# A four-layer graph transformer on one core: inverted places in the experts' routing, edge products awaited in twos, the output stored by tile

## What is computed

```python
xn = _layernorm(x)
x = x + gnn(xn, edges) + mix(xn)      # one kind of gnn and mix for each layer
x = x + ffn(_layernorm(x))

# layer 0's graph part
msg = edge_val[:, None] * (x @ W.T + b)[edge_col]
agg = segment_sum(msg, edge_row, num_segments=N)

# layer 3's feed-forward part (layer 1 likewise; layer 0 with one expert a node)
rw, re = top_k(softmax(tokens @ router_w.T), 2)      # weights and experts of a node
for e in range(8):
    h = gelu(tokens @ w1[e] + b1[e]); y = h @ w2[e] + b2[e]
    out = out + combine[:, e:e + 1] * y               # zero where e was not chosen
```

## Time and profile before

| | |
|---|---|
| time, median of 3 runs | 6284.4 us (6282.38 to 6292.41) |
| the profiled execution's own time | 6301.26 us |
| its span | 6299.3 us |
| mean granted TensorE clock | 0.798 of full speed |
| TensorE busy (matmul) | 4413.6 us, 70% |
| VectorE busy | 3201.3 us, 51% |
| GpSimd busy | 2895.1 us, 46% |
| ScalarE busy | 1234.3 us, 20% |
| DMA | 623.84 MB, mean 99 GB/s |

### The profile page before, as it was taken

One profiled execution on the slowest core, in us unless ns is written; L12 is line 12 of the kernel. 1 busy time (PEld: TensorE's weight loads), 2 busy tenths in 40 slices (PEclk: granted clock), 3 DMA queues, 4 the chain that ended last, 5 costly groups with the idle time before them and its releaser, 6 DMA issues. The chain is left out here.

```text
span 6299.3 us, 67353 instructions
## 1 busy us (share of the span) xinstructions
PE 4413.6 (70%) x17694; PEld 3077.6 (49%) x17694; DVE 3201.3 (51%) x7674; ACT 1234.3 (20%) x3062; POOL 2895.1 (46%) x2882
## 2 busy tenths in 40 slices
PE   0398857776796677665964937887399986777643
PEld 0246633333585454432444825566267763566542
DVE  7325545555002667777971145788722233577622
ACT  0022200001222110101142311100033342333211
POOL 1456656663101488774853046677100006566233
PEclk9998865556898775657986967988699998889776
DMA  4100013334011699885732224444300003222233
GB/s 154 50 6 2 2 54 92 91 92 112 28 34 58 200 288 284 272 265 159 222 103 74 69 75 121 107 111 112 69 1 0 0 22 102 76 86 87 70 105 106
DMA packets 411510, 623.84 MB, mean 99 GB/s; under 512 B 76713, under 2 KB 304446, under 8 KB 410789
## 3 DMA queue, kind: packets, MB, share of 16 engines
q0 software_dynamic: 124448, 324.61, 18.1%
q1 hardware_dynamic: 283588, 292.22, 14.8%
q10 hardware_dynamic: 3154, 3.20, 0.2%
HBM read 482.93 MB, written 137.50 MB: 98 GB/s over the span
## 5 line engine op out<-in xcount | busy, mean ns | idle before, releaser
L867 POOL DMA_INDIRECT m_rows<-support,far_at x440 | 447.6, 1017 | 1000.6 <-POOLq L126 748.8
L877 PE MATMUL g_sums_bank<-g_sums_rows,g_sums_same 128*125 128x256 f32 x880 | 459.2, 642 | 185.2 <-issue 171.1
L3855 POOL DMA_INDIRECT g_sp_rows<-h,src_at x440 | 467.4, 1062 | 220.1 <-issue 107.3
L3229 POOL DMA_INDIRECT g_sc_rows<-keyval,src_at x440 | 439.4, 999 | 238.1 <-issue 104.7
L522 POOL DMA_INDIRECT records<-record,place_at x416 | 419.2, 1008 | 281.2 <-issue 120.3
L867 POOL DMA_INDIRECT g_sums_rows<-h,far_at x440 | 415.6, 945 | 229.0 <-PE g_sums_bank L877 137.7
L3252 PE MATMUL g_sc_pair<-g1q_parts,g_sc_near 125*128 x1320 | 315.9, 366 | 191.5 <-DVE g_sc_rows L3296 134.9
L877 PEld LDWEIGHTS g_sums_bank<-g_sums_rows,g_sums_same 128*125 128x125 f32 x880 | 215.5, 292 | 428.8 <-issue 406.9
L3904 PE MATMUL g_sp_bank<-g_sp_rows,g_sp_same 128*125 128x264 f32 x880 | 309.6, 456 | 92.0 <-issue 49.0
L910 DVE TENSOR_TENSOR g_total<-g_total,g_sums_bank 125x256 f32 x440 | 184.6, 420 | 317.4 <-PE g_sums_bank L877 244.9
L936 PE MATMUL m_half<-m_rows,m_marks 128*125 128x256 f32 x880 | 254.8, 424 | 111.4 <-issue 72.3
(11 more groups left out here) (706 smaller groups left out, 9960.0 us busy)
## 6 DMA issues: line engine op xcount, KB each, us to landing
kept<-g_sc_rows SPq DMA_DIRECT2D x440, 128.0 KB
g_sp_rows<-kept SPq DMA_DIRECT2D x440, 128.0 KB
xnT<-sorted_rows SPq DMA_DIRECT2D x80, 256.0 KB
answer_rows<-f_answer SPq DMA_DIRECT2D x64, 256.0 KB
g_sc_kind_in<-kind_rows SPq DMA_DIRECT2D x55, 256.0 KB
g_sc_local_in<-local_rows SPq DMA_DIRECT2D x55, 250.0 KB
g_sp_local_in<-local_rows SPq DMA_DIRECT2D x55, 250.0 KB
answer_rows<-zero SPq DMA_DIRECT2D x1, 9856.0 KB
```

The costliest lines, as they stand in the source:

```text
L867: nc.gpsimd.indirect_dma_start(self.rows[:, k, :], None, self.table, bass.IndirectOffsetOnAxis(ap=core.far_at[:, s:s + 1], axis=0)).then_i ...
L877: nc.tensor.matmul(self.halves[s % slots], self.same[:, s % self.RING, :], self.rows[:, s % self.SLOTS, :], start=True, stop=True).then_in ...
L3229: nc.gpsimd.indirect_dma_start(rows[:, k, :], None, table, bass.IndirectOffsetOnAxis(ap=core.src_at[:, s:s + 1], axis=0)).then_inc(gathere ...
L3855: nc.gpsimd.indirect_dma_start(self.rows[:, k, :], None, self.table, bass.IndirectOffsetOnAxis(ap=core.src_at[:, s:s + 1], axis=0)).then_i ...
```

## The change

1. **Routing.** The places are inverted. A node's place is split into a block and a lane (VectorE); two sets of 0/1 masks are made, one over the blocks (`in_block`) and one over the 128 lanes (`in_lane`); GpSimd and ScalarE multiply the block masks by the tile's and the row's number (`spread_pool`, `row_act`); TensorE multiplies lane masks by these, 50 bf16 products for each choice (`invert_pe`), so that a bank holds for each lane and block the number of the node that belongs there. VectorE makes two integer lists of it (`to_at`, `from_at`), with spare rows for padding.
2. **Rows.** SP stores `xn` as it stands, by tile, into `sorted_rows` (now 3200 rows), five tiles at a time. In the experts' loop GpSimd gathers a step's rows in two indirect DMAs of 128, and scatters the answers in two, five steps later (LAG), to a region of `answer_rows` that lies by tile and choice. The scatters ahead of the loop and the gathers behind it are gone. Behind the loop SP loads 125 rows for each tile and choice in a plain DMA, into 16 buffers (8 in layer 0) in the memory of W1.
3. **The output** goes out from layer 3's last loop, one DMA of 125 rows for each tile once its two combines are done, eight tiles behind the loads; the phase `store` is gone.
4. **Layer 3's added rows** are added in five slices, one in each of the loop's first five steps.
5. **Layer 0's edge products** are waited for in twos: for a pair TensorE waits for the second matrix, for the add that frees the second bank, and for both gathers, and then issues both products. Banks, buffers and ring stay.
6. The zero fill covers 3200 and 14592 rows.

The diff, cut to its core:

```diff
+
+
+def tile_rows(table, first, count=1):
+
+    return table[first * W:(first + count) * W, :].rearrange("(t p) d -> p t d", p=W)[0:P]
...
-    def multiply(self, pe, s):
+    def multiply_two(self, pe, s):
         nc = self.core.nc
         slots = len(self.halves)
-        pe.wait_ge(self.matched, s + 1)
-        if s >= slots:
-            pe.wait_ge(self.added, s - slots + 1)
-        pe.wait_ge(self.gathered[s % self.SLOTS], 16 * (s // self.SLOTS + 1))
+        pe.wait_ge(self.matched, s + 2)
+        if s + 1 >= slots:
+            pe.wait_ge(self.added, s - slots + 2)
+        for i in (s, s + 1):
+            pe.wait_ge(self.gathered[i % self.SLOTS], 16 * (i // self.SLOTS + 1))
+        nc.tensor.matmul(self.halves[s % slots], self.same[:, s % self.RING, :], self.rows[:, s % self.SLOTS, :], start=True, stop=True).then_inc(self.summed, 1)
+        s += 1
         nc.tensor.matmul(self.halves[s % slots], self.same[:, s % self.RING, :], self.rows[:, s % self.SLOTS, :], start=True, stop=True).then_inc(self.summed, 1)
...
+        self.place, self.block, self.lane = (sb(n, [P, choices, NT]) for n in ("place", "block", "lane"))
+        self.tile_base = sb("tile_base", [P, choices * NT])
+        self.in_block, self.of_tile, self.of_row = (sb(n, [P, choices, NT, self.blocks], BF16) for n in ("in_block", "of_tile", "of_row"))
+        self.in_lane = lanes
...
+        self.started, self.picked, self.summed, self.tabled = (ph.sem(n) for n in ("started", "picked", "summed", "tabled"))
+        self.block_set, self.lane_set, self.tile_set, self.row_set, self.inverted, self.addressed = (
+            ph.sem(n) for n in ("block_set", "lane_set", "tile_set", "row_set", "inverted", "addressed"))
+
+    def spread_pool(self, pool):
         nc = self.core.nc
         for k in range(self.choices):
-            nc.gpsimd.iota(self.place_at[k][96:W], [[1, NT]], base=EXPERT_STEPS * EXPERT_ROWS + k * 32 * NT, channel_multiplier=NT).then_inc(self.started, 1)
+            pool.wait_ge(self.block_set, k + 1)
+            nc.gpsimd.tensor_tensor(self.of_tile[:, k], self.in_block[:, k], bcast_last(self.tile_base[:, k * NT:(k + 1) * NT], [P, NT, self.blocks]), ALU.mult).then_inc(self.tile_set, 1)
+
+    def row_act(self, act):
+        nc = self.core.nc
+        for k in range(self.choices):
+            act.wait_ge(self.block_set, k + 1)
+            nc.scalar.activation(self.of_row[:, k], self.in_block[:, k], ACT.Copy, scale=self.core.row[0:P, 0:1]).then_inc(self.row_set, 1)
+
+    def invert_pe(self, pe, bank):
+        nc = self.core.nc
+        last = self.choices * NT - 1
+        for k in range(self.choices):
+            pe.wait_ge(self.tile_set, k + 1)
+            pe.wait_ge(self.row_set, k + 1)
+            pe.wait_ge(self.lane_set, k + 1)
+            for t in range(NT):
+                n = k * NT + t
+                nc.tensor.matmul(bank[:, 0:self.blocks], self.in_lane[:, k, t, :], self.of_tile[:, k, t, :], start=n == 0, stop=False)
+                ins = nc.tensor.matmul(bank[:, 0:self.blocks], self.in_lane[:, k, t, :], self.of_row[:, k, t, :], start=False, stop=n == last)
+        ins.then_inc(self.inverted, 1)
+
+    def gather(self, pool, into, block, landed):
+        self.core.nc.gpsimd.indirect_dma_start(into, None, self.core.sorted_rows, bass.IndirectOffsetOnAxis(ap=self.from_at[:, block:block + 1], axis=0)).then_inc(landed, 16)
+
+    def scatter(self, pool, rows, block, landed):
+        self.core.nc.gpsimd.indirect_dma_start(self.core.answer_rows, bass.IndirectOffsetOnAxis(ap=self.to_at[:, block:block + 1], axis=0), rows, None).then_inc(landed, 16)
 
...
             link(nc.vector.tensor_tensor(self.equal[:], self.value[:], self.pick[k][:], ALU.mult))
-            link(nc.vector.tensor_reduce(self.place[k][:], self.equal[:].rearrange("p e t -> p t e"), AX.X, ALU.add))
-            nc.vector.tensor_copy(self.place_at[k][0:P], self.place[k][:]).then_inc(self.placed, 1)
+            link(nc.vector.tensor_reduce(self.place[:, k, :], self.equal[:].rearrange("p e t -> p t e"), AX.X, ALU.add))
+        link(nc.vector.tensor_scalar(self.block[:], self.place[:], 1.0 / W, -(W - 1) / (2.0 * W), ALU.mult, ALU.add))
+        link(nc.vector.tensor_scalar(self.block[:], self.block[:], ROUND, None, ALU.add))
+        link(nc.vector.tensor_scalar(self.block[:], self.block[:], ROUND, None, ALU.subtract))
+        link(nc.vector.scalar_tensor_tensor(self.lane[:], self.block[:], -float(W), self.place[:], ALU.mult, ALU.add))
+        wide, long = [P, NT, self.blocks], [P, NT, W]
+        for k in range(self.choices):
+            nc.vector.tensor_tensor(self.in_block[:, k], bcast_mid(core.ramp[0:P, 0:self.blocks], wide), bcast_last(self.block[:, k, :], wide), ALU.is_equal).then_inc(self.block_set, 1)
+        for k in range(self.choices):
+            nc.vector.tensor_tensor(self.in_lane[:, k], bcast_mid(core.ramp[0:P, :], long), bcast_last(self.lane[:, k, :], long), ALU.is_equal).then_inc(self.lane_set, 1)
         shape = [1, self.steps, EXPERTS]
         link(nc.vector.tensor_tensor(self.passed[:], bcast_mid(self.until[0:1, :], shape), bcast_last(core.ramp[0:1, 0:self.steps], shape), ALU.is_le))
         link(nc.vector.tensor_reduce(self.step_expert[:], self.passed[:], AX.X, ALU.add))
         link(nc.vector.tensor_scalar(self.step_expert[:], self.step_expert[:], float(EXPERTS - 1), None, ALU.min))
         nc.vector.tensor_copy(self.expert_at[:, 0:self.steps], self.step_expert[:]).then_inc(self.tabled, 1)
+        v.wait_ge(self.inverted, 1)
+        link(nc.vector.tensor_tensor(self.found[:], place_bank[:, 0:self.blocks], self.slot[:], ALU.max))
+        nc.vector.tensor_copy(self.to_at[:], self.found[:]).then_inc(self.addressed, 1)
+        link(nc.vector.tensor_scalar(self.slot[:], self.found[:], float(W * self.blocks), None, ALU.subtract))
+        if self.choices == 2:
+            link(nc.vector.tensor_scalar(self.fold[:], self.slot[:], float(W * NT), -float(W * NT), ALU.is_ge, ALU.mult))
+            link(nc.vector.tensor_tensor(self.slot[:], self.slot[:], self.fold[:], ALU.add))
+        link(nc.vector.scalar_tensor_tensor(self.fold[:], self.slot[:], -0.25, self.slot[:], ALU.mult, ALU.max))
+        nc.vector.tensor_copy(self.from_at[:], self.fold[:]).then_inc(self.addressed, 1)
...
                     sp.sem_inc(ph.spent, 1)
+            for g in range(NODE_LOOPS):
+                sp.wait_ge(norm.staged, (g + 1) * BODY)
+                sp.dma_start(tile_rows(core.sorted_rows, g * BODY, BODY), core.xn[:, g * BODY:(g + 1) * BODY, :]).then_inc(stored, 16)
             sp.wait_ge(loaded, nload)
-            sp.wait_ge(scattered, 16 * K * NT)
-            for i in range(LAST + 4):
-                if i < LAST:
-                    if i >= IN:
-                        sp.wait_ge(row_turned, i - IN + 1)
-                    sp.dma_start(rows[:, i % IN], core.sorted_rows[i * ROWS:(i + 1) * ROWS, :].rearrange("(j p) d -> p j d", p=128)).then_inc(row_in[i % IN], 16)
-                if i >= 4:
-                    s = i - 4
-                    sp.wait_ge(y_kept, s + 1)
-                    sp.dma_start(core.answer_rows[s * ROWS:(s + 1) * ROWS, :].rearrange("(j p) d -> p j d", p=128), answer[:, s % OUT]).then_inc(saved[s % OUT], 16)
-
-        @block.gpsimd
-        def _(pool):
-            route.spare(pool)
-            pool.wait_ge(route.placed, K)
-            for t in range(NT):
-                for k in range(K):
-                    nc.gpsimd.indirect_dma_start(core.sorted_rows, bass.IndirectOffsetOnAxis(ap=route.place_at[k][:, t:t + 1], axis=0),
-                                                 core.xw[:, t, :], None).then_inc(scattered, 16)
             for k in range(OUT):
-                pool.wait_ge(saved[k], 16 * len(range(k, LAST, OUT)))
+                sp.wait_ge(saved[k], 32 * len(range(k, LAST, OUT)))
             for n in range(K * NT):
                 t, k = n // K, n % K
                 if n >= BACK:
-                    pool.wait_ge(combined, n - BACK + 1)
-                nc.gpsimd.indirect_dma_start(back[:, n % BACK, :], None, core.answer_rows,
-                                             bass.IndirectOffsetOnAxis(ap=route.place_at[k][:, t:t + 1], axis=0)).then_inc(back_in[n % BACK], 16)
+                    sp.wait_ge(combined, n - BACK + 1)
+                sp.dma_start(back[:, n % BACK, :], tile_rows(core.answer_rows, route.blocks + k * NT + t)[:, 0, :]).then_inc(back_in[n % BACK], 16)
+                if out is not None and n >= BACK and (n - BACK) % K == K - 1:
+                    done = (n - BACK) // K
+                    sp.dma_start(nodes(out)[:, done, :], core.x[:, done, :]).then_inc(sent, 16)
+            if out is not None:
+                for t in range(NT - BACK // K, NT):
+                    sp.wait_ge(combined, K * (t + 1))
+                    sp.dma_start(nodes(out)[:, t, :], core.x[:, t, :]).then_inc(sent, 16)
+                sp.wait_ge(sent, 16 * NT)
+
+        @block.gpsimd
```

(35 more changed lines are left out.)

125 lines of the change are left out of this document (68 added, 57 removed).

## The result

The changed kernel takes 6202.6 us, median of 4 runs (6196.35 to 6209.09), against 6286.6 for the one before on the same chip (4 runs, 6282.38 to 6292.41): a ratio of 0.9872, 95% interval 0.9858 to 0.9887. That is 84 us less. The forecast was 152 less (6132), the range reached from 6098 to 6220. The time lies in the range, at the place of the second case, in which the pairing of layer 0's products does nothing (6207). The upper end of the range came from that case, not from the forecast's own sum (6100 to 6165).

The account below looks back on a forecast made before the run. The prediction found no engine full and took layer 0's matmul-to-add turn as its edge stage's pace. Gains of 75 (pairing), 19 (layer 0's experts), 41 (layer 1) and 17 (layer 3) made 152, so 6132 us; range 6098 to 6220.

Parts of the forecast that it names:

- the forecast's own sum: Whole kernel: 152 us gained, median 6132, own range about 6100 to 6165; chance 0.50.
- The pairing: Layer 0's edge products awaited in twos: 1.31 us a step or GpSimd's 1.25, 67 to 88 gained, 75 taken.
- the step that named the bound: Layer 0's edge stage: the turn from matmul to add and back, 1.43 to 1.45 us, sets the pace, not GpSimd.
- the first rival: Layer 0's edge stage: pairing does nothing, since a pair repeats the memory or semaphore turn; 6207, chance 0.22.
- the sign of being wrong: Layer 0's edge stage: the forecast is wrong if the stage keeps 1.46 us a step.
- Layer 3's head: Last reduce to TensorE's first rows in layer 3: 32.9 us against 74.3, 41 gained.
- Layer 3's loop: Layer 3's experts' loop: four GpSimd transfers bind at 5.05 us a step; 8 allowed for clock dips, 3 for slices.
- a rival of 72 for a clock that falls: Layer 3's experts' loop: GpSimd starves TensorE, slow clock, 7.3 us a step, 72 more, 6204; chance 0.10.
- Tails: After the experts' loops: plain 125-row copies at 1.07 us each; layer 3's tail 27 gained.
- The rival in which the copies use all engines: Tails end at VectorE's pace, some 50 us earlier in layer 3 and 25 in layer 1: 6057, chance 0.04.
- Layers 0 and 1's experts: Inverted routing in both: 19 us gained in layer 0 (12 to 22), 41 in layer 1 (30 to 50).
- The slower case: Layer 0's edge stage: six products in flight for seven, 7/6 as long, 107 us more, 6314; chance 0.06.

Follow-up runs that it names:

- the first pair: The kernel before and the changed kernel, measured and profiled first, on one chip: 6286.6 and 6202.6 us, ratio 0.9872.
- the quick kind: Chips on which the unchanged kernel before takes 5982 to 5985 us; there the whole change measured ratio 0.982.
- the first kind: Chips on which the unchanged kernel before takes 6282 to 6303 us; there the whole change measured ratio 0.9872.
- the run with it at 0.95 and more work: Changed kernel with layer 0's products issued twice, layer 3's experts' loop turns three times, and 128-row tail copies: 6129.5 us, ratio 0.9766 to the kernel before.
- the 128-row run: Changed kernel with the plain copies behind the three experts' loops bringing 128 rows each in place of 125: 5796.5 us, ratio 0.9686 to the kernel before.

## Why the prediction was right or wrong

**The pairing: wrong, by the step that named the bound.** The total fell into the range by the first rival, not by the forecast. I read "TensorE's next product starts 0.10 after an add" and "six steps ahead" as a turn of 1.43 us, and took a part of the turn away. A product that waits for a bank starts after an add whatever makes the adds late. The rows that spoke against it were in the trace: an add may run as soon as one of six finished products is signalled, so with six ahead by their records it isn't the products' start that is late but their signal. I put half the chance nevertheless on 75. Measured: -4.4 in the first pair, +1.9 on the quick kind, and nothing when it is undone there; a step takes 639.4/440 = 1.45 us, which is the sign of being wrong that I had set. The first rival named the outcome and its size (6207 for 6203), with the turn's repetition as its reason, which the runs don't bear out: on the quick kind there is no turn at all, 1.27 us a step is GpSimd's own pace, and the most that anything on TensorE could have given was the 84 us down to it. That 6207 and 6203 lie so near is luck: layer 3 gave 17 less than worked out, and the stages ahead of layer 0's experts and the untouched stretch made it up.

**Layer 3's head: better than the sum.** First rows of TensorE at 26.2 after the last reduce in place of 32.9:

```profile
5887.97 0.57 DVE L1533 TENSOR_REDUCE f_place<-f_equal 125x25 f32<-125x200 f32 x1
...
5891.47 10.38 POOL L1455 TENSOR_TENSOR f_of_tile<-f_in_block,f_tile_base 125x1600 bf16<-125x1600 bf16 x2 [97.78 <-DVE f_in_block L1540]
5892.97 12.23 DVE L1542 TENSOR_TENSOR xnT<-ramp,f_lane 125x3200 bf16<-125x3200 f32 x2
...
5908.47 0.19 DVE L1550 CAST f_to_at<-f_found 128x64 int32<-128x64 f32 x1
...
5910.50 0.99 POOL L1477 DMA_INDIRECT xnT<-sorted_rows,f_from_at  x1 [8.65 <-DVE f_from_at L1556]
...
5914.70 1.09 PE L1806 MATMUL f_bank<-ident,xnT 128*128 128x128 f32 x4 [6.53 <-DMA xnT<-sorted_rows,f_from_at]
```

The masks end at 5905.20, 15.7 after the small ops, where I had 10.2 + 6.5 in series. In series is what the trace shows, though the rows overlap: a row's time holds its wait for the other engine. The second block mask ends at 5893.05 and the first multiply 2.72 later, at 5895.77; the first lane mask ends 3.35 after that, the second multiply 2.73 after the mask, the second lane mask 3.35 after the multiply. So a lane mask of 6.15 by its row is 3.35 of work (3.4 in the sum), and a multiply of 4.3 or 6.1 is 2.7 (3.3 in the sum). Layer 0's experts show the same with one choice:

```profile
1686.12 0.99 DVE L1540 TENSOR_TENSOR f_in_block<-ramp,f_block 125x800 bf16<-125x800 f32 x1
1687.03 3.48 DVE L1542 TENSOR_TENSOR f_hid<-ramp,f_lane 125x3200 bf16<-125x3200 f32 x1
...
1687.27 4.64 POOL L1455 TENSOR_TENSOR f_of_tile<-f_in_block,f_tile_base 125x800 bf16<-125x800 bf16 x1 [203.74 <-DVE f_in_block L1540]
1690.43 1.75 DVE L1544 TENSOR_TENSOR f_passed<-f_until,ramp 1x256 f32<-1x256 f32 x1
```

The mask came first and took its 3.48; the multiply of half the size ends 1.40 after it, and VectorE's next op, 0.41 in layer 3, takes 1.75. The mis-sized term of the head is the second choice's 50 products: 3.0 us, 0.053 each, for the 9.5 that I had from 0.19 each. The row that I took it from has 128 columns at half clock among waits.

**Layer 3's loop: the mechanism right, its size only on the quick kind.** Four transfers a step bind the loop: 171.8 on the quick kind for 164.5, 1.32 a transfer for 1.26. On the first kind 196.0. I had 8 us "for dips of the clock", and a rival of 72 for a clock that falls. The clock did dip (0.89), but the run with it at 0.95 and more work was as long; the 24 us more than on the quick kind go with the late signals, which only the first kind has. From the last reduce to the last answer it is 202.7 before and 214.6 after: the head gained 48 for the 41 worked out, the loop gave back 60, and the tail gained 12. So layer 3 as a whole gave 0.1 for the 17 worked out, and 23.3 on the quick kind.

**Tails: right.** 1.15 to 1.17 us a copy for 1.07, at the bound of 1.16 that I had, on a third of the engines as worked out. The rival in which the copies use all engines (6057) fell, and the 128-row run shows what it would have been worth.

**Layers 0 and 1's experts: right,** 20.3 for 19 and 43.9 for 41, and within 0.5 the same on both kinds: 20.5 and 43.9. The parts came less well than the sums. In layer 1 TensorE's first rows stand 26.2 after the last reduce in place of 68.4, 42 gained for 35, by the small products again; the loop gave 1.4 of it back and the tail gained 3 for 6. In layer 0 the head gained 22 for 17, and some 4 went again in the loop.

**The slower case** (two free banks for a pair, 107 us) fell. Pairs leave six products in flight in place of seven, and the stage didn't get 7/6 as long (639.4 for 643.7), so what holds it isn't a fixed delay of each product.

What stays open is why TensorE's signals come late on one kind of chip. Shown is where: beside GpSimd's transfers, when TensorE doesn't set the pace; that the clock and the stage's shape don't decide it; and that twice the work doesn't cure it. Whether it is the gaps or GpSimd's rate (one transfer per 1.5 us late, per 1.8 punctual) wasn't told apart, and a loop with GpSimd's transfers thinned but TensorE still waiting wasn't tried. Every time here comes from an execution that was recorded, so no run shows whether the recording has a part in it. The untouched stretch between layers 1 and 3 is 179 us longer on the first kind, 2284.6 against 2105.3 in the kernel before, and the traces show late signals in it: between 3850 and 4350, 340 of the 658 of TensorE on record come over 0.2 us late, on the quick kind (3700 to 4150) none of 775. That they cost the 179 us is argued from this, not shown. The same holds for the start up to layer 0's first gather, 863.8 against 804.4.
